# The sixth pair's shared experts issued ahead of the sorted experts' tiles in a six-part decoder kernel

## The reference, cut to what matters

```
shared_out = _swiglu(x, ws_gate, ws_up, ws_down)          # every token, hidden width 256
scores = sigmoid(x @ gate_weight.T)                       # 8 experts
topk_w, topk_idx = top_k(scores, 2); topk_w = 2.5 * topk_w / topk_w.sum(-1)
y[t, e] = swiglu(x[t], w_gate[e], w_up[e], w_down[e])     # hidden width 128
out[t] = sum_k topk_w[t, k] * y[t, topk_idx[t, k]] + shared_out[t]
x = x + out
```

## Time and profile before

| what | value |
|---|---|
| median of three runs | 805.96 us (805.84 to 806.11) |
| the profiled execution, its own time | 808.89 us |
| the profiled execution, its span (first to last instruction) | 807.1 us |
| PE busy | 771.3 us, 96% |
| DVE busy | 502.7 us, 62% |
| granted PE clock, mean | 0.994 of full speed |
| last block's tiles, in the trace | from 716.2 us to 783.9 us |

### The profile page before, as it was taken

The page is one execution under the profiler, slowest core; times in us unless marked ns, Lnnn a source line. Parts: engine busy times, 40 slices in busy tenths (PEclk is TensorE's granted clock), DMA queues, the critical chain, the costliest instruction groups (busy, mean ns, idle before and its releaser), DMA issues.

```text
span 807.1 us, 16936 instructions
## 1 busy us (share of the span) xinstructions
PE 771.3 (96%) x6093; PEld 624.1 (77%) x6093; DVE 502.7 (62%) x1386; ACT 422.6 (52%) x1254; POOL 312.7 (39%) x441
## 2 busy tenths in 40 slices
PE   7999999999999999999999999999999989999998
PEld 6887777777788888877777777777777767878876
DVE  4675677677622343147667766677788886566655
ACT  2445677677532223337776766666655676423320
POOL 3232222222233222323222226566678744616550
PEclk9999999999999999999999999999999999999999
DMA  8902233422052236000000003000000001235538
GB/s 315 374 2 73 73 81 112 100 73 74 1 144 73 73 80 138 14 0 2 2 1 2 1 2 118 15 14 15 14 15 28 27 28 39 81 85 166 159 118 312
DMA packets 57569, 61.46 MB, mean 76 GB/s; under 512 B 21296, under 2 KB 48176, under 8 KB 56464
## 3 DMA queue, kind: packets, MB, share of 16 engines
q1 hardware_dynamic: 54080, 51.03, 21.2%
q0 software_dynamic: 3408, 9.34, 3.4%
HBM read 31.10 MB, written 29.27 MB: 75 GB/s over the span
## 4 chain that ended last, share of the span: by engine, by line
PE 65%; ACT 11%; DVE 7%; POOL 6%; issue 5%; DMA 2%; another core or an unknown queue 1%; SPq 1%; POOLq 0%; DVEq 0%
PE pj L368 11%; PE pj L361 8%; PE pj L454 8%; PE ov L530 7%; PE sc L517 7%; ACT pr L1461 6%; PE sc L443 6%; POOL routed_y L1721 5%; PE ov L465 4%; PE sc L438 3%; PE pj L355 3%; DVE mx L980 2%; PE ov L368 2%; ACT qT L1468 1%
## 5 line engine op out<-in xcount | busy, mean ns | idle before, releaser
L1461 ACT ACTIVATE pr<-sc,mx 128x128 f32<-128x128 f32 x768 | 214.6, 414 | 84.3 <-DVE mx L980 84.3
L980 DVE TENSOR_REDUCE mx<-sc 128x4 f32<-128x512 f32 x192 | 119.2, 683 | 41.1 <-PE sc L443 41.0
L454 PE MATMUL pj<-idn,pr 128*128 128x128 f32 x768 | 120.5, 281 | 15.2 <-ACT pr L1461 10.7
L454 PEld LDWEIGHTS pj<-idn,pr 128*128 128x128 f32 x768 | 88.1, 143 | 42.6 <-issue 20.0
L987 DVE COPY pT<-pj 128x512 f32<-128x512 f32 x128 | 87.3, 686 | 38.0 <-PE pj L454 37.4
L1647 POOL TENSOR_SCALAR ve<-mv 128x2 f32<-128x2 f32 x40 | 14.1, 351 | 191.0 <-DVE mv L926 190.0
L1479 ACT ACTIVATE hT<-sc,vecs 128x256 f32<-128x256 f32 x64 | 30.4, 474 | 90.6 <-PE sc L517 90.6
L517 PE MATMUL sc<-xnT,W 128*128 128x256 f32 x256 | 64.1, 380 | 0.0
L530 PE MATMUL ov<-W,hT 128*128 128x256 f32 x256 | 60.5, 381 | 0.0
L1663 POOL TENSOR_SCALAR kM<-kraw,vecs 128x256 f32<-128x256 f32 x64 | 34.8, 558 | 62.5 <-ACT kraw L1447 62.5
L443 PE MATMUL sc<-kM,qT 32*128 32x256 f32 x768 | 55.0, 400 | 0.2 <-ACT hT L1479 0.2
(11 more groups left out here) (225 smaller groups left out, 1522.9 us busy)
## 6 DMA issues: line engine op xcount, KB each, us to landing
sorted_x<-more_xT SPq DMA_DIRECT2D x15, 1152.0 KB, 7.6
kM<-sorted_x SPq DMA_DIRECT2D x39, 129.0 KB
cT<-in_ctxT SPq DMA_DIRECT2D x16, 256.0 KB, 3.4
W<-in_w SPq DMA_DIRECT2D x2, 1024.0 KB, 12.8
cT<-in_ctx SPq DMA_DIRECT2D x8, 256.0 KB, 3.0
W<-in_w_gu SPq DMA_DIRECT2D x1, 2048.0 KB, 9.0
hT<-routed_y SPq DMA_DIRECT2D x8, 256.0 KB, 6.0
out_x<-X SPq DMA_DIRECT2D x8, 256.0 KB, 4.0
```

The source lines that it names most:

```text
L454: last = tr(bank[b][:, i * S:(i + 1) * S], pr[n % 4][:, i, :], idn[:])
L980: v.tensor_reduce(mx[n % 4][:], four(b), AX.X, ALU.max, negate=True).then_inc(mx_done, 1)
L1461: last = a(pr[n % 4][:, i, :], bank[b][:, i * S:(i + 1) * S], ACT.Exp, bias=mx[n % 4][:, i:i + 1])
```

## The change

`AHEAD` goes from 5 to 6. Pair 5 thereby becomes a pair ahead: its `shared_up` and `shared_down` stand before the tiles, its routed rows are added by four `routed_added` of DVE in place of PE's products with four diagonals, and there are 8 diagonals in place of 12. SP reads pair 5's routed rows last and writes pair 5 out last. ACT's silu calls follow the same constant.

```
-AHEAD = 5
+AHEAD = 6
...
             shared_up(4, 0)
             shared_up(4, 1)
             shared_down(3)
+            shared_up(5, 0)
+            shared_up(5, 1)
             shared_down(4)
+            shared_down(5)
             pe.wait_ge(tab_done, 3)
...
             shared_added(3)
+            shared_gated(5, 0)
+            shared_gated(5, 1)
             shared_added(4)
+            shared_added(5)
             shares()
...
-            shared_gated(5, 0)
-            shared_gated(5, 1)
             shared_gated(6, 0)
             shared_gated(6, 1)
             pair_added(0)
...
             pair_added(2)
             pair_added(3)
-            shared_added(5)
+            shared_added(6)
             pair_added(4)
-            shared_added(6)
             shared_added(7)
+            pair_added(5)
...
-            for b in (2 * p + j for p in (0, 1, 5, 2, 6, 3, 7, 4) for j in two):
+            for b in (2 * p + j for p in (0, 1, 2, 6, 3, 7, 4, 5) for j in two):
...
-            for p in (0, 1, 2, 3, 5, 4, 6, 7):
+            for p in (0, 1, 2, 3, 6, 4, 7, 5):
```

## The result

| kernel, five runs each | median | range |
|---|---|---|
| before | 805.96 us | 803.16 to 806.33 |
| changed | 810.66 us | 807.91 to 811.12 |

The ratio is 1.0055, with a 95% interval from 1.0034 to 1.0077: the change costs 4.4 us by the ratio (2.7 to 6.2), 4.7 by the medians.

The account below looks back on a forecast made before the run. PE's own list bounds the start of the tiles; the end hangs on the `routed_y` reads and PE after them. 805.96 + 5.0 ahead + 1.3 at the end = 812.2 us; own range 811.2 to 813.5, with rivals 810.3 to 814.0.

Parts of the forecast that it names:

- PE's own list starts the tiles, and the added matmuls cost 5.2 us: Ahead of the first tile: its rows are already in SBUF, so 12 more PE matmuls delay it by 5.2 us.
- DVE's two diagonals less give 0.2 us back: At the first tile's gate: DVE makes four diagonals, not six, removing PE's 0.21 us idle time before the first `turn_hidden`.
- The work removed from the tail turns into a wait of 5.4 us: Behind the tiles: PE sheds 7 us of work but waits 5.4 us for pair 6's first read, landing at 795.36.
- The low clock costs 1.7 us on PE and 1.3 at the end: Behind PE's tail wait: clock at 0.50 costs PE 1.7 us; DVE's last additions end 1.3 us later than before.
- The forecast for a full clock: Behind the tiles, no clock loss: PE ends at 801.6, DVE at 804.2, tail 0.4 us shorter.
- Sum: +6.3: Whole kernel: +5.0 us ahead of the tiles and +1.3 us at the end, giving 812.2 us; chance 0.62.
- its own range: Whole kernel time, forecast with the clock's cost included: 811.2 to 813.5 us, chance 0.62.
- the rival's range: Whole kernel time if the low clock harms nothing: 810.3 to 811.1 us, chance 0.21.
- The rival of a harmless clock: Behind PE's tail wait: low clock only inside the wait, or none; 810.6 us, chance 0.21.
- The rival of a new wait ahead of the tiles: At `shared_down(5)`: ACT's silu comes 2 to 4 us late and PE stands; 814.2 to 816.2 us, chance 0.10.
- the idle 1.48 us ahead of `shared_down(3)`: Ahead of the tiles: PE waits for DVE's `shared_added(2)`; the added rows stand behind this gap and can't fill it.

Follow-up runs that it names:

- the fourth experiment: Changed kernel with `shared_up(5, 0)` ahead of `shared_down(3)` in place of behind it; median 813.10 us, ratio to before 1.0052.
- the first experiment: The changed kernel run again, unaltered, against the kernel before; median 814.99 us, ratio to before 1.0083.
- the second experiment: Changed kernel with 11 unread matmuls on PE in its wait for pair 6's routed rows; median 813.46 us, ratio to before 1.0061.

## Why the prediction was right

- *PE's own list starts the tiles, and the added matmuls cost 5.2 us.* Measured 5.18 us between the two traces that are alike there, 5.08 in the other. Adding such matmuls and nothing else puts 5.18 us ahead of the first tile and costs 5.8 us (4.3 to 7.1). Shown.
- *DVE's two diagonals less give 0.2 us back.* The first `turn_hidden` comes 0.21 us sooner behind the first tile. As said.
- *The work removed from the tail turns into a wait of 5.4 us, since the reads land 0.67 us apart.* 5.60, 5.27 and, in the fourth experiment, 5.50 us. With pair 5's shared work left in its place, the wait is 0.5 us and the tail is no shorter than before (20.0 us): PE's work there costs the tail nothing.
- *The low clock costs 1.7 us on PE and 1.3 at the end.* DVE's end was forecast 18.7 us behind the first read (805.9 - 787.23) and came at 18.82 and 18.30. With PE kept busy it is 16.86 and 16.94, where 17.0 was forecast for full clock. The tails were 21.3, 20.8 and 21.7 us with the low clock and 19.7 twice without, so the clock cost 1.1 to 2.0 us of tail in these traces, and the times moved by 1.5 and 2.0 us. The mechanism is shown; its size varies with the execution. The forecast for a full clock, a tail 0.4 us below the 19.9 of before, is nearly met as well (0.2 below).
- *Sum: +6.3.* The first measurement has +4.7, the first experiment +6.1 for the same kernels. The first ratio's interval ends at +6.2, just under the forecast, and 810.66 us is outside the 811.2 to 813.5 that I had given the forecast as its own range. It is inside 810.3 to 814.0 only because that took in the rival's range; this part is luck. The stretches of the two traces do add up to the forecast (5.08 - 0.21 ahead, 1.4 in the tail, 6.3 in all). Why five runs differ by 4.7 is open; one kernel's executions spread over 5 to 6 us on the other chips. Adding the parts by the medians of the experiments: 5.8 (work ahead) - 1.3 (rows by DVE) + 1.5 (clock) = 6.0, against 6.1 measured. Each part is uncertain by 1 us or more, so such a close fit is luck too.

The rival of a harmless clock (810.6) is nearest to the first median of 810.66, and yet it is not what happened: both traces of the changed kernel have the low clock, and so has that of the fourth experiment with the same tail. A time alone would have picked the wrong case. The Trainium skill (page "TensorE: Matmul & The Clock Gate", section "HAM oscillation — how this bites in real kernels") describes this as waits for DMA after which PE starts cold each time; here it is one such wait at the end of a kernel, and rows at 0.50 stand behind it in both traces. The rival of a new wait ahead of the tiles did not happen either: in these three traces PE is never idle between the start of `shared_down(3)` and the first tile.

One reading was too narrow. I treated the idle 1.48 us ahead of `shared_down(3)` as lost to the change, which holds for the order as written. In five more traces it is there again (1.5 to 2.5 us), in two it is not (the changed kernel's first, and the second experiment's), and one `shared_up` put into it costs nothing. That is where the change could have been had for 1.9 us less.

No version beats the kernel before by more than can be measured. The best, pair 5's rows by DVE alone, is at -1.3 us with an interval across zero.

## What to carry to other kernels

Work that was moved off a stretch full of DMA came back as a wait of the engine that it was taken from; read first how far apart the transfers land, and count what the engine would still have to wait for. A wait of PE just ahead of the last matmuls (5.3 to 5.6 us here) can cost a second time by the clock behind it, and unread matmuls in the wait were a cheap repair. When two profiled executions are compared, measure each stretch from a point of its own: here the changed kernel's span was shorter by 1 us, and the kernel was slower by 4.7 by the medians.

## What the runs showed that I had not expected

PE's waits and the clock behind them. Ahead of `shared_down(3)` and in the tail, waits of 0.5 to 1.5 us (0.68, 0.74, 0.82, 1.48, 1.50, 1.51) left it at full speed; behind 2.18, 2.19, 2.51, 2.88, 5.27 and 5.60 us it was at 0.50 for 3 to 4 us, and behind 5.50 us for 4.8. The length of a wait does not decide by itself: near 17 us, at the same wait in every trace, 2.44, 2.55, 2.73 and 2.92 us left the clock at full speed, while it fell behind 2.30, 2.87 and 3.05 to 3.74 us. At 199 us in the trace of before, it fell behind a wait of only 0.90 us between small products. So a wait of 2 to 3 us may or may not bring the low clock, and each place has to be looked up in its own trace.

Between about 696 and 708 us, ACT and DVE see PE's signals up to 5 us behind the recorded ends of its matmuls (the totals: 703.05, seen at 708.01), and the trace names no releaser. DVE starts the table 4.1 to 5.0 us behind the end of the totals in eight of the ten traces. In the two others, the changed kernel's first and the second experiment's, it is 0.7 and 0.9 us, and just these two have `shared_down(3)` start without a wait in the unchanged order. So the late table very likely makes the idle time there. What delays the signals stays open. POOL issues its last scatters meanwhile, but it does so beside the totals in the changed kernel's first trace too, where nothing is late; no run takes the scatters out of that stretch.
